# The opening of a fused attention and expert kernel: four moves and one step by chunk

## The reference

```
x = x + (x @ W[subject].T + b[subject])
x = x + zX * lap_x(x) + zY * lap_y(x) + zR * x * (1 - x)
x = x + attention(x, side)       # 16 heads of 16; keys from x, queries from side, one own key for each token
x = x + experts(x)               # chosen expert and two shared ones, 256 -> 1024 -> 256, relu, weighted by a softmax gate
```

## Time and profile before

| | us |
|---|---|
| median of 3 runs | 1003.73 |
| the runs | 1002.61 to 1004.05 |
| the profiled execution's own time | 1004.07 |
| its span, first to last instruction | 1002.2 |
| opening, until `H0` of image 0 | 74.17 |
| TensorE busy over the span | 97% |
| VectorE, ScalarE, GpSimd busy | 79%, 68%, 64% |

### The profile page before, as it was taken

How to read it: one execution, slowest core, us unless ns; L and a number is a source line. 1 busy time by engine, 2 the same in 40 slices (tenths; PEclk the granted TensorE clock), 3 DMA queues, 4 the chain that set the end, 5 groups by cost and what they waited for, 6 DMA issues and landing times.

```text
span 1002.2 us, 28010 instructions
## 1 busy us (share of the span) xinstructions
PE 975.7 (97%) x9631; PEld 928.5 (93%) x9631; DVE 795.1 (79%) x1565; ACT 684.4 (68%) x1440; POOL 636.4 (64%) x545
## 2 busy tenths in 40 slices
PE   8889999999999999999999999999999999999897
PEld 7679999999999999999999999999999999999897
DVE  6877888878888787878888788888878878788644
ACT  4776858677685876768577685866768586676642
POOL 4867747576585757658565774856668475765441
PEclk9989999999999999999999999999999999999999
DMA  7433131223213222331322223122331312231110
GB/s 213 136 106 107 60 113 61 63 84 105 85 43 109 80 63 84 86 103 42 95 83 76 84 69 111 53 74 76 103 84 58 111 63 63 84 101 58 44 54 11
DMA packets 92044, 82.70 MB, mean 83 GB/s; under 512 B 12116, under 2 KB 90996, under 8 KB 92020
## 3 DMA queue, kind: packets, MB, share of 16 engines
q1 hardware_dynamic: 91588, 81.99, 27.9%
q10 hardware_dynamic: 432, 0.39, 0.1%
HBM read 52.59 MB, written 4.20 MB: 57 GB/s over the span
## 4 chain that ended last, share of the span: by engine, by line
PE 49%; POOL 23%; issue 20%; DVE 3%; ACT 3%; DMA 1%; SPq 1%; POOLq 0%; ACTq 0%
POOL prob_lo L1547 7%; POOL exp_lo L1483 6%; PE out L712 5%; PE out L714 5%; PE out L713 5%; PE hid L712 5%; PE hid L713 4%; PE hid L714 4%; PE front L712 3%; PE front L838 3%; PE front L714 3%; PE front L713 3%; PE front L824 2%; PE pv L779 2%; POOL p_lo L1500 1%
## 5 line engine op out<-in xcount | busy, mean ns | idle before, releaser
L712 PE MATMUL hid<-x_hi,exp_hi 128*128 128x256 f32 x768 | 230.4, 300 | 0.5 <-DVE x_lo L1331 0.5
L1547 POOL TENSOR_TENSOR prob_lo<-prob,prob_hi 128x512 f16<-128x512 f32 x142 | 183.7, 1294 | 68.9 <-ACT prob_hi L1097 68.6
L712 PE MATMUL out<-hid_hi,exp_hi 128*128 128x256 f32 x768 | 226.5, 295 | 0.0
L1483 POOL TENSOR_TENSOR exp_lo<-raw,exp_hi 128x512 fp32r<-128x512 f32 x128 | 169.0, 1335 | 82.7 <-ACT exp_hi L1114 82.5
L713 PE MATMUL hid<-x_lo,exp_hi 128*128 128x256 f32 x768 | 216.2, 281 | 0.0
L714 PE MATMUL hid<-x_hi,exp_lo 128*128 128x256 f32 x768 | 215.6, 281 | 0.0
L713 PE MATMUL out<-hid_lo,exp_hi 128*128 128x256 f32 x768 | 214.5, 279 | 0.0
L714 PE MATMUL out<-hid_hi,exp_lo 128*128 128x256 f32 x768 | 214.4, 279 | 0.0
L1256 DVE TENSOR_REDUCE s_max<-front 128x2 f32<-128x512 f32 x247 | 163.3, 688 | 62.4 <-PE front L824 60.5
L1136 ACT ACTIVATE hid_hi<-hid 128x512 fp32r<-128x512 f32 x192 | 115.1, 599 | 96.5 <-PE hid L714 94.7
L1093 ACT ACTIVATE prob<-front 128x512 f32<-128x512 f32 x246 | 147.9, 601 | 24.7 <-PE front L838 23.0
(11 more groups left out here) (262 smaller groups left out, 2335.2 us busy)
## 6 DMA issues: line engine op xcount, KB each, us to landing
raw<-in_wi SPq DMA_DIRECT2D x64, 256.0 KB, 3.8
raw<-in_wo SPq DMA_DIRECT2D x64, 256.0 KB, 2.8
q_rows<-w_raw SPq DMA_DIRECT2D x80, 128.0 KB, 2.4
k_rows<-x_raw SPq DMA_DIRECT2D x48, 128.0 KB, 2.4
k_rows<-x1T SPq DMA_DIRECT2D x45, 128.0 KB, 2.4
x_raw<-in_x SPq DMA_DIRECT2D x16, 256.0 KB, 2.9
w_raw<-in_w SPq DMA_DIRECT2D x16, 256.0 KB, 2.7
s_raw<-in_side SPq DMA_DIRECT2D x16, 256.0 KB, 3.7
```

What stands on the lines that cost most here:

```text
L712: nc.tensor.matmul(acc, w_hi, a_hi, start=first, stop=False)
L1483: nc.gpsimd.tensor_tensor(lo, source, hi.bitcast(F32), ALU.subtract).then_inc(w_split, 1)
L1547: nc.gpsimd.tensor_tensor(prob_lo[:, h % NPROB, :], prob[:, h % NPROB, :], prob_hi[:, h % NPROB, :], ALU.subtract).then_inc(prob_split_poo ...
```

## The change

It touches the opening alone; the loop's and the closing part's lists stay as they are.

1. ScalarE rounds shared quarter 4 before `E0` and not after `E1`.
2. VectorE makes the low part of shared quarter 4 after head 11's low part, and not before `half`; so `half` comes first.
3. TensorE runs `E8` before `q.1`; a fill of two stays behind `E9`. The two stages change places in the ring of banks too.
4. GpSimd runs `norm` before head 12's low part.
5. x3 of image 0 is made by chunk of 128 features: `wo` puts chunk 0 in the second PSUM bank and chunk 1 in the first and signals each; `x3T`, the high and the low part follow in halves; `H0` starts when chunk 0's low part is there, and waits for chunk 1's after three matmuls.

```
 OPEN_PE
-E6 lap.1 E7 q.1 E8 fill2 E9 kp.1 E10 fill2 E11 ...
+E6 lap.1 E7 E8 q.1 E9 fill2 kp.1 E10 fill2 E11 ...
 OPEN_ACT
-shared2 shared3 w_parts.1 x_parts.1 s_parts.1 m0 E0 E1 shared4 E2 E3 ...
+shared2 shared3 w_parts.1 x_parts.1 s_parts.1 m0 shared4 E0 E1 E2 E3 ...
 OPEN_DVE
-shared2 E7 shared4 half kp.1 E11 E13 E14 E15 att k3.1 aT wo x3_parts vp.1 self.1
+shared2 E7 half kp.1 E11 shared4 E13 E14 E15 att k3.1 aT wo x3_parts vp.1 self.1
 OPEN_POOL
-E12 norm qa.1 qb.1 after_att shared5 ...
+norm E12 qa.1 qb.1 after_att shared5 ...
+X3_ALONE = (0,)
...
 hidden(s, j)
                 if s == 0:
-                    wait(pe, x3_split, 1, j, 1)
+                    if alone(j):
+                        pe.wait_ge(x3_lo_first, X3_ALONE.index(j) + 1)
+                    else:
+                        wait(pe, x3_split, 1, j, 1)
...
                     for k in range(C):
+                        if alone(j) and (s, f, k) == (0, 0, 1):
+                            wait(pe, x3_split, 1, j, 1)
...
 TensorE, wo
+                    if alone(j):
+                        w_hi, w_lo = linear(3)
+                        for c in range(C):
+                            for k in range(C):
+                                at = slice(c * P, (c + 1) * P)
+                                last = product(pv_bank[1 - c][:, 0:S], w_hi[:, k, at], w_lo[:, k, at], ak_hi[:, k, :], ak_lo[:, k, :],
+                                               k == 0, k == C - 1)
+                            last.then_inc((wo_first, wo_done)[c], 1)
...
 VectorE, wo
+                    for c in range(C):
+                        if c == 0:
+                            dve.wait_ge(wo_first, X3_ALONE.index(j) + 1)
+                        else:
+                            wait(dve, wo_done, 1, j, 1)
+                        nc.vector.tensor_tensor(x3T[:, c, :], pv_bank[1 - c][:, 0:S], x2b[:, c, :], ALU.add
+                                                ).then_inc((x3_first, x3_done)[c], 1)
```

More of the change, by code:

```diff
@@ L116 @@
 S0 S1 S2 S3 fill4 S4 S5 fill4 S6 S7 fill4 S8 S9 S10 fill4 m0 S11 S12 fill4 S13 S14 fill8 E0 S15 E1 x1.1 E2 fill2 E3 fill2 E4 m1 fill2 E5
-E6 lap.1 E7 q.1 E8 fill2 E9 kp.1 E10 fill2 E11 fill2 E12 fill2 E13 fill3 E14 fill3 E15 fill6
+E6 lap.1 E7 E8 q.1 E9 fill2 kp.1 E10 fill2 E11 fill2 E12 fill2 E13 fill3 E14 fill3 E15 fill6
 pvend vs.1 fill6 aT ks.1 wo vp.1 self.1
@@ L121 @@
 x_parts w_parts s_parts lin0 x1_parts react lin1 lin2 x2_parts q qa lin3 kp qb k0 kq ks vs shared0 vp shared1 x2b
-shared2 shared3 w_parts.1 x_parts.1 s_parts.1 m0 E0 E1 shared4 E2 E3 x1_parts.1 react.1 E4 m1 E5 E6 E7 x2_parts.1 E8
+shared2 shared3 w_parts.1 x_parts.1 s_parts.1 m0 shared4 E0 E1 E2 E3 x1_parts.1 react.1 E4 m1 E5 E6 E7 x2_parts.1 E8
 E9 q.1 qa.1 E10 kp.1 E11 E12 E13 E14 E15 qb.1 kq.1 shared5 aT vs.1 ks.1 shared6 x3_parts vp.1 shared7 x2b.1
@@ L131 @@
 memsets lin0 lin1 qa lin2 qb lin3 ks shared0 shared1 vp shared3a maxima shared3b w_parts.1 x_parts.1 s_parts.1 E0 E2 x1.1 E4 m1 E6 E8 E9 E10
-E12 norm qa.1 qb.1 after_att shared5 ks.1 after_x3 shared6 vp.1 shared7
+norm E12 qa.1 qb.1 after_att shared5 ks.1 after_x3 shared6 vp.1 shared7
 """))
@@ L218, with alone @@
 BQ, BK, BO, BV, B_PREV, B_SELF, NVEC = range(7)
+X3_ALONE = (0,)
+def alone(j):
+    return isinstance(j, int) and j in X3_ALONE
 LINKS = {"early": 3, "attention": 4 + 5 + len(HI_DVE), "rest": 8}
@@ L434, in build @@
         stored = sem("stored")
+        wo_first = sem("wo_first")
+        x3_first = sem("x3_first")
+        x3_hi_first = sem("x3_hi_first")
+        x3_lo_first = sem("x3_lo_first")
         y_cols_done = sem("y_cols_done")
@@ L903, in rest @@
                     wait(pe, att_split, 1, j, 1)
-                    feature_major(pv_bank[1], linear(3), ak_hi, ak_lo).then_inc(wo_done, 1)
+                    if alone(j):
[7 more added lines that the diff above has]
+                    else:
+                        feature_major(pv_bank[1], linear(3), ak_hi, ak_lo).then_inc(wo_done, 1)
                 elif name[0] == "H":
@@ L1141, in rest @@
                     nc.scalar.activation(gate_s[:, 4:7], gate_s[:, 1:4], ACT.Exp).then_inc(gate_exp, 1)
+                elif name == "x3_parts" and alone(j):
+                    for c in range(C):
+                        if c == 0:
+                            act.wait_ge(x3_first, X3_ALONE.index(j) + 1)
+                        else:
+                            wait(act, x3_done, 1, j, 1)
+                        nc.scalar.activation(x3_hi[:, c, :], x3T[:, c, :], ACT.Copy).then_inc((x3_hi_first, x3_hi_done)[c], 1)
                 elif name == "x3_parts":
@@ L1323, in rest @@
                     nc.vector.scalar_tensor_tensor(y, y, gate_s[:, 9:10], x3_kept[:, :, :], ALU.mult, ALU.add).then_inc(chosen_added, 1)
+                elif name == "wo" and alone(j):
+                    wait(dve, x2b_done, 1, j, 1)
+                    wait(dve, x3_copied, 1, j, 0)
+                    for c in range(C):
+                        if c == 0:
+                            dve.wait_ge(wo_first, X3_ALONE.index(j) + 1)
+                        else:
+                            wait(dve, wo_done, 1, j, 1)
+                        nc.vector.tensor_tensor(x3T[:, c, :], pv_bank[1 - c][:, 0:S], x2b[:, c, :], ALU.add
+                                                ).then_inc((x3_first, x3_done)[c], 1)
+                elif name == "x3_parts" and alone(j):
+                    for c in range(C):
+                        if c == 0:
+                            dve.wait_ge(x3_hi_first, X3_ALONE.index(j) + 1)
+                        else:
+                            wait(dve, x3_hi_done, 1, j, 1)
+                        nc.vector.tensor_tensor(x3_lo[:, c, :], x3T[:, c, :], x3_hi[:, c, :].bitcast(F32), ALU.subtract
+                                                ).then_inc((x3_lo_first, x3_split)[c], 1)
                 elif name == "wo":
```

## The result

The changed kernel takes 1005.65 us (median of 15 runs, 1003.33 to 1007.12), the kernel before 1003.43 (15 runs, 1001.88 to 1004.79). The ratio is 1.0028, 95% interval 1.0021 to 1.0035: slower by 0.28%. The forecast was 1003.1 with a range to 1005.3; the result lies outside it, beside rival C's 1005.9. As a difference the forecast was -0.95 us and the measured one is +2.2.

What follows compares the result with a forecast made beforehand. TensorE's own work bounds the loop, so the opening's gain or loss moves the end. Terms -0.15 - 0.1 - 0.7 sum to -0.95: 1004.07 - 0.95 = 1003.1 us, range 1001.1 to 1005.3.

Steps and rivals of the forecast that it cites:

- rival C: Opening: TensorE stands for heads 13 to 15 and its clock falls at 63 to 68; +1.85, 1005.9 us; chance 0.18.
- Up to head 8's values: Opening: late `q.1`, then `half` at 55.0 and head 8's values at 56.2 in place of 57.52, -1.3 us.
- its -0.2: ScalarE before `E0`: early roundings hide in idle time, stages to `lap.1` and head 5's low part come 0.2 us earlier.
- The turns of VectorE and GpSimd: Opening, from about 57 us: instructions of the two engines wait for each other; VectorE's end 0.54 us after GpSimd's.
- both hang on 0.2 us, I take the middle, -0.15: Head 15's low part: +0.35 us if `qb.1` gets its turn, -0.65 if head 15 is ahead; priced at -0.15.
- the chain from the last values to `wo` keeps its length, if the clock stays: Opening behind the last heads: nothing is edited until `wo`, so no change in length was priced.
- Its first half: VectorE's `half` ahead of quarter 4: starts at 55.0 in place of 56.29, head 8's values come 1.3 us earlier.
- Edit 3's price of 1.3: TensorE's `q.1` behind `E8` starts 1.7 us later; what `half` waits for comes 1.3 us later.
- the second half: VectorE makes quarter 4's two pieces between head 11 and heads 13 to 15; priced with edit 4 at -0.15 us.
- Edit 5's term: Behind `H0`: x3 by chunk brings SyncE's transfers, and the maxima TensorE awaits, 0.7 us earlier: -0.7, bounds -0.92 and 0.
- The cover of SyncE: SyncE's later `wi_load` delays the keys to 76.0; `S0` needs them at 77.12, leaving 1.1 us of cover.

Runs made afterwards that it cites:

- holding the clock with fills: Changed kernel plus 28 fill matmuls in TensorE's waits for the last heads, against the kernel before: 1006.09 us, ratio 1.0018 [1.0009, 1.0027].
- the repeated run: The changed kernel timed again without alteration in a later session, against the kernel before: 1007.06 us, ratio 1.0032 [1.0019, 1.0044].

## Why the prediction was wrong

**Up to head 8's values it held.** Forecast and trace: `q.1` at 49.0 and 49.46, head 7's values 54.6 and 54.37, `half` 55.0 and 54.78, head 8's values 56.2 and 56.03. The low rate of `q.1` was right (0.21 us a matmul for most of it). One thing in edit 3 was missed: `E8` needs the transfer of the maxima's rows, which `q.1` used to cover, and TensorE stands 0.69 us for it at 48.32. It cost nothing that showed, as head 5's low part ended only 0.23 us after those scores.

**Edit 1** hid, but its -0.2 does not show. `E0`'s exponentials start at 37.41 behind 1.68 us of idle time, so the roundings took 1.04 of the 2.72, yet head 5's low part starts at 48.31 against 48.12. No run has edit 1 alone.

**The turns of VectorE and GpSimd were right; the middle between two outcomes was wrong.** The step "both hang on 0.2 us, I take the middle, -0.15". Quarter 4 ran from 58.76 to 61.20 (58.7 to 61.05 forecast), `qb.1` started at 62.96 (62.8), got its turn, and head 15 ended at 64.93 (64.8): +0.48 against 64.45. With `qb.1` in its turn the same step said +0.35. It is the rule, too: in the five kernels with edits 2 and 4 the three last heads take 3.81 to 3.83 us. The mean of two outcomes was not one of the outcomes; here it hid that one of the two branches made the part a loss. It is 0.63 us of the error.

**The clock was the largest error that the traces place.** The step "the chain from the last values to `wo` keeps its length, if the clock stays" priced it at nothing and left it to rival C at 0.18. The rows already spoke against: TensorE stands between 60 and 65 for a VectorE that the same text had slowed down. In the changed kernel `den` to transposes is 3.55 and 3.77 in place of 2.70, so the price is 0.85 to 1.07 at this place, and holding the clock with fills brings 2.70 back. Rival C had 1.3 for it, added 1 for the matmuls behind, and came to 1005.9; measured 1005.65. The 1 isn't borne out: transposes to `H0` got shorter, not longer (5.90 and 6.19 against 6.55). What stands in its place is the stretch ahead of `half`: in the repeated run the clock is 0.50 from 44 to 52 and `half` starts at 56.32, 1.5 later than in the first (0.7 of it since head 5's low part starts later). So C's mechanism is shown, and its number is right in part by compensation. Of the 3.2 us between -0.95 and +2.2 the clock (0.85 to 1.07) and the middle (0.63) are 1.5 to 1.7, less 0.3 that edit 5 won beyond its term; the rest, more than half, stays open.

**Which edit.** Undoing edit 2 takes the whole loss back (0.9997 against 1.0028 and 1.0032). Its first half did what the prediction said: with edit 3 undone or left out, the way to `half` is 2.3 us shorter. Edit 3's price of 1.3 was about right as well (1.5 between the means of the table, 1.08 for head 7's values in the first trace), and it is paid out of that gain. What was priced by a middle is the second half, the same two pieces behind `half`: +2.3, as VectorE is what TensorE waits for there and its subtractions alternate with GpSimd's. With both edits the way from head 5 to `att` is -2.3 + 1.5 + 2.3 = +1.5 longer and the clock adds 0.85 to 1.07: +2.4 to +2.6 at the transposes, less 1.1 for edit 5: +1.3 to +1.5. That is the upper side: it adds the clock to a mean in which three kernels have 3.5 to the transposes for another reason. By whole sums, which count nothing twice, it is 20.8 against 19.0, +1.8, less 1.1: +0.7; and the changed kernel's two traces against the one of before (20.65 and 21.70 against 19.50, less 1.1) give +0.05 and +1.1. The medians say 2.2 and, in the repeated run, 2.7. So the sign and the places are shown, and of the size at most two thirds; the rest is not. The start of head 5's low part varies enough from trace to trace to hold it, but no run shows that it does.

**Edit 5's term** was -0.7 with bounds -0.92 and 0. The last column says -1.1, and the 0.92 us wait is gone or down to 0.2 to 0.6. It came from where the step put it, behind `H0`. **The cover of SyncE** held: the chosen expert's load went at 61.40 (61.2 forecast), the keys' row was issued at 71.27, and `S0` at 77.79 did not wait.

The Trainium skill (GPSIMD Engine Reference, section Specifications) names the contention with VectorE's instructions of two inputs, and this case agrees: 1.65 and 1.64 us for heads 13 and 15 beside GpSimd's instructions, against 0.68 for head 14 between them.

Not tried: the two pieces left out altogether, which would tell the collision from the pieces' own 1.28 us. Edit 4's part is open (ratio 1.0020 without it, 9.17 in place of 9.67 us to `att`; the last three heads take 3.25 in place of 3.81).

## What to carry to other kernels

- Work moved from one place on the critical chain to another on the same chain wins nothing, however long the wait that it leaves behind: 2.3 us won before `half` were 2.3 us lost behind it. And a second edit can spend the slack that the first one counts on, as edit 3 does with the way to `half`; time them alone and together.
- Where a forecast makes TensorE run ahead and stand, price the matmuls behind that stand at both clocks, and take no average between two outcomes.
- Where runs of one kernel spread by 3 us, take ten or more, and read the stages' lengths, not their start times, from several traces. Here one trace for each kernel left more than half of the error unplaced.

## What the runs showed of the hardware that I had not expected

- Waits of about 1 us each, with TensorE busy 1.17, 0.75 and 1.01 of three stretches of 2 us, were followed by a granted clock of 0.50 at 66 to 68 us. With edit 5 alone, a wait of 1.24 us before head 15's values (63.70), with TensorE busy 2.76 of the 4 us around it, was followed by 1.00 at 64 to 68. So the length of the last wait alone did not tell.
- VectorE and GpSimd took turns over 6 us: subtractions of two float32 inputs of 128x512 took 1.64 or 1.65 on VectorE where one of GpSimd's of that size had begun before them, 0.68 where GpSimd was idle, and 1.60 on GpSimd against 1.16 alone. The merged rows (2.44 for two, 3.81 for three) hide that. VectorE's sums from PSUM in `att` took 1.09 for two both with GpSimd's `qa.1` beside the first of them (only edit 3, 65.09) and with GpSimd idle (changed kernel, 65.79).
- Between two kernels a higher mean clock did not mean a faster one: 0.9946 with 1004.07 us against 0.9935 with 1002.73.
